# Decoder layer with a sparse memory attention: one more quarter of a step's weights computed on ScalarE

## What is computed

```python
def entmax15(x):
    x = (x - max(x)) / 2
    ...                                  # tau: the threshold for which the weights sum to 1
    return square(clip(x - tau, 0))
...
Q = layernorm(hidden) @ Wq.T
for _ in range(3):
    scores = einsum("bhsd,hnd->bhsn", xi, K) * beta
    w = entmax15(scores)
    xi = einsum("bhsn,hnd->bhsd", w, V)
out = xi @ Wo.T
x = layernorm(x + attn(x)); x = layernorm(x + xattn(x, ctx)); x = layernorm(x + ffn(x))
```

## Time and profile before

| | |
|---|---|
| median of 3 runs | 906.6 us (906.1 to 909.6) |
| profiled execution | 906.5 us, span 904.6 us |
| PE busy | 834.2 us, 92% of the span |
| DVE busy | 794.6 us, 88% |
| ACT busy | 705.6 us, 78% |
| POOL busy | 494.3 us, 55% |
| chain that ended last | PE 65%, DVE 18%, ACT 7%, POOL 5% |

### The profile page before, as it was taken

The page is one execution under the profiler, slowest core; times in us unless marked ns, Lnnn a source line. Parts: engine busy times, 40 slices in busy tenths (PEclk is TensorE's granted clock), DMA queues, the critical chain, the costliest instruction groups (busy, mean ns, idle before and its releaser), DMA issues.

```text
span 904.6 us, 17069 instructions
## 1 busy us (share of the span) xinstructions
PE 834.2 (92%) x4958; PEld 719.5 (80%) x4958; DVE 794.6 (88%) x2051; ACT 705.6 (78%) x1691; POOL 494.3 (55%) x2306
## 2 busy tenths in 40 slices
PE   6999996899999999999999999999999997999961
PEld 5877785688888888888888888888888886887850
DVE  3699999999999999999999999999998998978431
ACT  3588897998888989878989697989697789866320
POOL 4133536664564656666656566575645557654423
PEclk9999999999999999999999999999999998999995
DMA  8900020000000000000000001000000000000000
GB/s 280 204 1 1 16 91 11 9 2 2 1 1 1 1 1 13 1 3 1 1 1 1 12 2 30 7 1 1 2 1 19 1 1 7 7 1 7 7 1 27
DMA packets 24212, 17.55 MB, mean 19 GB/s; under 512 B 11761, under 2 KB 23537, under 8 KB 23857
## 3 DMA queue, kind: packets, MB, share of 16 engines
q1 hardware_dynamic: 23872, 16.13, 6.3%
q0 software_dynamic: 240, 0.27, 0.2%
HBM read 14.30 MB, written 2.10 MB: 18 GB/s over the span
## 4 chain that ended last, share of the span: by engine, by line
PE 65%; DVE 18%; ACT 7%; POOL 5%; issue 3%; DMA 1%; SPq 0%; POOLq 0%
PE banks L1227 24%; PE banks L1250 11%; DVE moments L793 7%; PE banks L1238 6%; PE banks L1278 6%; PE banks L1311 4%; PE banks L1101 4%; DVE top L773 4%; ACT work L704 3%; PE banks L1287 3%; DVE work L813 2%; PE banks L1303 2%; ACT work L695 1%; ACT work L716 1%; PE banks L1324 1%
## 5 line engine op out<-in xcount | busy, mean ns | idle before, releaser
L793 DVE BATCH_NORM_STATS2 moments<-work 128x6 f32<-128x512 f32 x576 | 373.7, 686 | 5.8 <-ACT work L704 2.9
L704 ACT ACTIVATE work<-work,neg_u 128x256 f32<-128x256 f32 x768 | 329.1, 519 | 47.5 <-DVE neg_u L805 25.6
L1227 PE MATMUL banks<-weights_s,work 128*128 128x256 f32 x1536 | 350.7, 381 | 6.1 <-ACT work L695 4.2
L1227 PEld LDWEIGHTS banks<-weights_s,work 128*128 128x128 f32 x1536 | 286.9, 191 | 46.2 <-issue 7.6
L695 ACT ACTIVATE work<-banks,neg_low 128x256 f32<-128x256 f32 x384 | 152.7, 494 | 10.2 <-DVE neg_low L784 10.0
L923 POOL TENSOR_TENSOR resid_sum<-moments 128x8 f32<-128x8 f32 x144 | 30.7, 214 | 226.6 <-DVE moments L793 225.4
L773 DVE MAX8 top<-banks 128x8 f32<-128x256 f32 x384 | 141.7, 415 | 8.2 <-PE banks L1227 7.4
L716 ACT ACTIVATE work<-banks 128x512 f32<-128x512 f32 x192 | 112.9, 611 | 24.4 <-PE banks L1238 23.9
L1238 PE MATMUL banks<-ident,work 128*128 128x128 f32 x768 | 107.9, 276 | 15.0 <-DVE work L813 7.5
L1250 PE MATMUL banks<-weights_s,work 128*128 128x256 f32 x512 | 115.0, 380 | 0.3 <-ACT work L716 0.3
L1238 PEld LDWEIGHTS banks<-ident,work 128*128 128x128 f32 x768 | 86.2, 141 | 31.9 <-DVE work L813 16.1
(11 more groups left out here) (155 smaller groups left out, 1154.2 us busy)
## 6 DMA issues: line engine op xcount, KB each, us to landing
work<-in_L_xattn_Wo_dram SPq DMA_DIRECT2D x2, 1024.0 KB, 11.0
out_dram<-work SPq DMA_DIRECT2D x16, 128.0 KB, 1.7
work<-in_L_xattn_w_kc_q_dram SPq DMA_DIRECT2D x2, 768.0 KB, 5.5
rows<-in_L_xattn_Wq_dram SPq DMA_DIRECT2D x1, 1536.0 KB, 13.8
rows<-in_x_dram SPq DMA_DIRECT2D x1, 1536.0 KB, 7.1
work<-in_L_attn_Wq_dram SPq DMA_DIRECT2D x1, 1024.0 KB, 10.3
work<-in_L_attn_Wo_dram SPq DMA_DIRECT2D x1, 1024.0 KB, 13.6
work<-in_ctx_dram SPq DMA_DIRECT2D x32, 32.0 KB, 2.2
```

What stands on the lines that cost most here:

```text
L704: ins = nc.scalar.activation(q_resid[:, j, h, :], q_resid0[:, j, h, :], ACT.Relu, bias=small["neg_u"][:, j, h:h + 1])
L793: ins = nc.vector.bn_stats(moments[:, j, 2 * q:2 * q + 2, :].rearrange("p h k -> p (h k)"), r.rearrange("p h n -> p n h"))
L1227: ins = nc.tensor.matmul(ps_scores[:, h, :], lhsT, w[:, h, t, :], start=(t == 0), stop=(t == CT - 1))
```

## The change

A constant `DVE_WEIGHTS = 2` takes the place of the fixed three. DVE computes the quarters 0 and 1 of the weights (heads 0 to 3), ACT the quarters 2 and 3 (heads 4 to 7), in one stage `last_weights` of four instructions with a signal after each quarter. PE waits for the third quarter on ACT's semaphore. The strings of all engines are replaced; that of DVE is 48 entries shorter (one for each of 16 tiles and 3 steps). Lines behind the new constant are three higher, and behind `last_weights` four.

```diff
+DVE_WEIGHTS = 2
...
-        dve += four("weights", s)[:3]
+        dve += four("weights", s)[:DVE_WEIGHTS]
...
-        "SP": "3015249876304ac2db157f6e89abdecf",
+        "SP": "023156741a92806c3bef45d78ac9bedf",
...
-            RESID_STEP = (EVALS - 1) * QUARTERS + 1
+            RESID_STEP = EVALS * QUARTERS - DVE_WEIGHTS
...
                         act.wait_ge(u_ready[j], eval_count(p, s, EVALS - 1))
-                        for h in (6, 7):
+                        for h in range(2 * DVE_WEIGHTS, HEADS):
                             ins = nc.scalar.activation(q_resid[:, j, h, :], q_resid0[:, j, h, :], ACT.Relu,
                                                        bias=small["neg_u"][:, j, h:h + 1])
-                        ins.then_inc(resid_ready[j], 1)
+                            if h % 2:
+                                ins.then_inc(resid_ready[j], 1)
...
-                        if q < 3:
-                            pe.wait_ge(weights_ready[j], p * (STEPS * 3) + (s * 3 + q + 1))
+                        if q < DVE_WEIGHTS:
+                            pe.wait_ge(weights_ready[j], p * (STEPS * DVE_WEIGHTS) + (s * DVE_WEIGHTS + q + 1))
                         else:
-                            pe.wait_ge(resid_ready[j], resid_count(p, s, EVALS, 1))
+                            pe.wait_ge(resid_ready[j], resid_count(p, s, EVALS, q - DVE_WEIGHTS + 1))
```

More of the change, by code:

```diff
@@ L177, in tile_turns @@
     return {
[L178 to L211, removed]
@@ new lines, in tile_turns @@
+        "ACT": "hhhhhhhh01h000000h02101h110h0h00hh2h2h1h11h100022h11011h02221h0h20h010121h0200120h2h11131h000211h021"
+               "21h333232h11h1303h33h1202h2023h33322h2h2100133331000042235000021233336020010373323211021132330300111"
+               "1220223111122203342444102304434142112442144330330204144555504343555005323422544455254453343431556266"
+               "6535661636801335515563646644456556567777461565777114467535166674754626669275547122445456766772575567"
+               "524a264424b77677643444667473474475355456367762776553535347375888748545588458866686843884999965647494"
+               "99987669c9988797878795665698896886777878885475887aaaa989867ada855a5a599e78899aa8aa97899967aa76a77999"
+               "898688596899bbbb8a88a9bbbbaaaa887bbb66b68689abaf8ba7ab8788999a9a8aa9a9996aac7c7cbbc9998bb797bcb7a7c9"
+               "cacbbbb9a8ac9c9aabbbb9ccaacba8bbaccddddc9c8aa8ad7d8cad8d8c8bccddddacc9bdac9caddaccccabbbbcc8eecee9db"
+               "bdb9ebae99e9e9bbbbdddedeaeebccadedbdbedebdbddcdcccda9ddeffffadadbffffaaafddffdfedfbcbeffccacefefebcb"
+               "ccfffcfbebebebecfffcfecceeedddcdeffeeffdedddbefcdfecdfceddeecdceeceeccdceeeeffedffdefeefddffceffdddd"
+               "ffffeeeffffeedfeeeefffffefffff",
@@ new lines, in tile_turns @@
+        "POOL": "hh0000101100112221120200010212101133303322211323hhhh200000202333003311113231212201124244442420140333"
+                "5355553444553243636604065656564145757713757665616176722444466044577744555727535327475588861666883456"
+                "96499889966997273778884787486a5aa885aa79997aa93958998885bbb878bb66aabab88aa9949a9a69698c77cc99bbbcc5"
+                "bbaaabaccb9ada7dd88addccacdd7cc6cc8babbeb8ee99bbeebdbdede9dd7ddbaf9ffaffcfcfccaacecedebbffccfeedd8df"
+                "eefdbdcffdbdeee9eccdeeeefcfffddaffecffdbedefeeffgcfefdf",
```

28 lines of the change are left out of this document (23 added, 5 removed).

## The result

| | before | changed |
|---|---|---|
| median, 4 runs each | 907.25 us (906.13 to 909.62) | 916.3 us (915.46 to 917.18) |
| ratio | | 1.0096 (95%: 1.0072 to 1.0120) |
| profiled execution, span | 906.5, 904.6 us | 915.5, 913.7 us |
| granted clock, whole span | 0.981 | 0.976 |

The account below looks back on a forecast made before the run. PE was taken as nearly full, held up in the middle mostly by DVE's long queue. The terms -3.4 + 2.5 - 0.6 - 2.7 - 1.4 = -5.6 took the profiled 906.5 us to 901 us, range 890 to 915.

Parts of the forecast that it names:

- ACT in the middle: From 200 to 700 us ACT's load rises from 86.2% to 91.8%, adding 2.5 us of PE waits.
- Moved entries: Rewritten lists of PE, ACT, POOL and SP, mostly moved by one to five entries, costed at nothing.
- the idle time moves by over 5 us at a place where weights play no part: Sign that the forecast is wrong and the rewritten lists, not the moved quarter, made the difference.
- The third quarter: PE's waits before third quarters (heads 4 and 5) in the middle go: -3.4 us, bounds 0 and -11.5.
- the five places: Five PE waits before a third quarter, from 277.48 to 657.19 us, 3.4 us together.
- the -0.6: The rest of PE's waits for DVE in the middle, 2.6 us, shrinks with DVE's load by 0.6 us.
- The start: From 50 to 200 us half of DVE's relief of 5.4 us reaches PE: -2.7 us.
- late: From 700 to 850 us a fifth of 7.5 us of POOL waits and lost clock is gained: -1.4 us.
- rival C: DVE's relief reaches further, idle share at start and late falls to the middle's: 886 us, chance 0.05.
- The durations: Expected profile: L817 x192 about 60 us, L714 x192 about 87; DVE about 765 us busy, ACT 749.
- B: Longer ACT blocks become PE's wait: 913 us, chance 0.24; sign: PE waits for ACT of over 10 us.
- A: Nothing to be felt, ACT's cost meets the third quarter's saving: 905 us, 902 to 911, chance 0.29.

Follow-up runs that it names:

- e1: The new split of two quarters on DVE and two on ACT, with the lists of the kernel before; 919.33 us, 1.0131.
- e8: The kernel before with DVE's third quarter left out, ACT's load and the lists unchanged; 903.75 us, 0.9969.
- e7: The kernel before with two unused relu added behind ACT's quarter in each of the 48 blocks; 919.35 us, 1.0162.
- e12: The kernel before with one unused relu added behind ACT's quarter in each block; 910.49 us, 1.0038.
- e13: The kernel before with ACT's fourth quarter left out, all lists unchanged; 908.31 us, 1.0017.
- e14: The changed kernel with the third quarter left out on ACT, so new lists with two quarters on DVE and one on ACT; 915.81 us, 1.0103.
- e2: The old split of three quarters on DVE and one on ACT, with the changed kernel's lists; 926.0 us, 1.0202.
- e9: The kernel before with five third quarters that PE waited for moved right behind their second on DVE; 906.73 us, 0.9997.
- e10: The kernel before with the third quarter of five steps that PE waited for computed on ACT instead of DVE; 907.45 us, 1.0004.
- e3: The changed kernel with tile 11's softmax sums and tile 12's second quarter moved earlier in DVE's list; 917.35 us, 1.0115.
- e6: The changed kernel with ACT's block of four split in two entries, the first square between them; 933.51 us, 1.0317.
- e11: The kernel before with two unused relu per step added behind ACT's fourth square instead of in the block; 920.48 us, 1.0146.

## Why the prediction was wrong

The time of 916.3 us lies outside the range of 890 to 915. Step by step:

- **"ACT in the middle", +2.5.** This is the term that failed first. Without the moved entries, the prediction's terms are worked out on the order of before, and their sum is -5.6; e1 is that kernel and took 12.1 us more than before (919.33 against 907.26). The gains were put at 8.1 us and came to 2.9 (e8). The load on ACT was put at 2.5 in the middle and at nothing elsewhere. It cost 12.7 us by the medians, 14.7 by the ratio (e7). In the middle alone, from PE's 1010th matmul to its 3952nd, e7's profiled execution took 509.9 us against 501.4, so the term of 2.5 measured 8.5; 3.8 us of waiting for the square that PE needs became 12.1 from 50 to 850 us. The value came from a line through two engines' busy shares and waits, which treats 91.8% as the cause of a wait. It isn't one: half the load cost a quarter (e12), 36 us less gave nothing (e13), and on the new lists the same load cost nothing that shows (e14). The line's two waits were also read low, from the two largest lines of each engine; over all lines of 200 to 700 us they are 4.1 us for ACT and 7.0 for DVE, which would have given +1.7, further off still.
- **"Moved entries. ... I cost them at nothing."** This step failed as well. At equal load the rewritten lists cost 12 us with 2 and 1 quarters (e14 against e8) and 18.7 with 3 and 1 (e2), and gave back 3 with the changed kernel's own 2 and 2 (e1 against the changed kernel). The step looked only at POOL and at transfers, and took "by one to five entries" for small. The rewrite did away with the price of ACT's load and put one of its own in its place, so the changed kernel is slow for another reason than e1. The prediction named a sign for this, "the idle time moves by over 5 us at a place where weights play no part". It came near: the waits outside the turn of the weights rose by 4.6 us, 4.1 of them for L772.
- **The third quarter, -3.4.** The wait was read rightly and it went, but the value is wrong. In the changed kernel ACT has all four relu of tile 10 done 19 us before PE gets there, and PE waits 0.34 us, for a square; no wait for the weights of a third quarter is left:

```profile
494.65 1.73 ACT L714 ACTIVATE work<-work,neg_u 128x256 f32<-128x256 f32 x4
...
515.83 1.11 PE L1242 MATMUL banks<-ident,work 128*128 128x128 f32 x8 [0.34 <-ACT work L720]
```

  At the five places together PE still waits 1.8 us ahead of the third quarter in the changed kernel, for the square or the copy that frees the bank, and 0.6 ahead of tile 6's second. Moved alone the five quarters give 0 (e9, e10); with the relief of DVE all 48 give 2.9 (e8), of which the middle shows 3.0 between the same two matmuls (498.4 us), where this term and the -0.6 had 4.0. The text had it as a bound, "0 (the next wait takes its place)", and that end was the true one for the places alone.
- **The start, -2.7, and late, -1.4.** Both wrong. In e8 PE's 1010th matmul starts at 201.0 us, against 200.3: the relief gives nothing in the start. From its 3952nd to its 4801st the relief gives 0.6 us (146.5 against 147.1). In the changed kernel the idle time from 50 to 200 us rose from 14.2 to 15.4, and late the clock fell to 0.95. The largest wait in each was known not to be for weights; that argument, put under rival C, spoke for setting these terms to nothing.
- **The durations.** L817 took 60.3 us for 60 forecast. L714 took 82.0 for 87: 0.427 us each in blocks of four, where the pairs had 0.455. DVE came to 773.0 us for 765 and ACT to 741.4 for 749: both moved by less than their groups (21.6 and 35.8 us against 29.7 and 38.4). None of this bears on the result.
- **The rivals.** B gave 913 us and the right sign, with a chance of 0.24. Its mechanism and its price (14.6 us, less the gains) are what the old lists show (e1, e7), but it isn't what holds the changed kernel, so that 913 is near 916.3 is luck. Its sign, waits for ACT of over 10 us, is met (6.7 + 3.6 + 1.3 = 11.6), but the kernel before had 9.2 of the same kinds and e14, with ACT's load gone, keeps the two larger lines at 9.2. It was no test. A and C are ruled out.
- **The skill.** The Trainium skill, ScalarE: Activation LUTs, section Rules for kernel authors, says of a relu "Use VectorE, not ScalarE", and the change goes against it. The trace agrees on the ranking of the durations, 0.427 against 0.314 us (82.0 and 60.3 us by 192), and the estimate of 0.40 us was near. The result has the rule's sign. With the old lists the added relu on ScalarE did cost 1.6% (e7); with the lists of the change they cost nothing that shows (e14), and that kernel is slow for another reason.

What stays open: which engine's list carries the 12 us of e14 against e8. Exchanging the list of one engine alone wasn't tried. PE's waits give a hint: ahead of a second quarter it waits 4.5 us for DVE's weight in e14, 0.2 in the kernel before. Nor is it shown that no good order exists for the new split; e1, the changed kernel and e3 to e6 are six orders, all slower than before, by 1.0 to 3.2%. In the old order the relief of DVE gives 0.3% (e8); by that estimate a third quarter on POOL, which wasn't tried either, would give no more there. No version here that computes all the weights beats the kernel before.

## What to carry to other kernels

Where each engine works through a fixed list, an engine's busy share doesn't say what its next microsecond costs: ACT was 78% busy, and 34.5 us more cost 13 to 15 us, half of that about 3, and 36 us less gave nothing. Price a move of work by running the two halves apart, the relief with the work left out and the load with a dummy added, before the order is rewritten; here these two runs show a gain of 0.3% and a cost of 1.6% on the old order. And when the change also rewrites the order, cross orders and loads in a table. The two need not add, and a table with one corner missing can name a cause that the other corner takes back: e14 alone says the order costs 1.3%, e1 that at the change's own load it costs nothing.

## What the runs showed of the hardware that was not expected

- A stall can be paid twice. The changed kernel's PE stands still 4.6 us longer and is busy 4.5 us longer for the same 4958 matmuls, while the granted clock is below 1.00 in 50 of the 100 us around its large waits (before in 20). Many short waits did not do this: e7's PE stands still 9.9 us longer (80.3 against 70.4), 8.3 of them in waits of at most 1.7 us for the square, and is busy only 2.0 us longer, with the clock of the span at 0.980 (before 0.981). In e11 PE is busy 841.9 us, 7.7 more than before, though no wait stands out; its clock of 0.977 accounts for about half of that, and the rest is not explained.
- One instruction more costs its engine less than its own time. A DVE weight of 128x256 has a mean of 362 ns in its row and 0.3125 us as its share of the group, since neighbours overlap, but 96 fewer took only 0.21 to 0.23 us each off DVE's busy time (e8: 20.5 us, the change: 21.6). This last figure is rough: with the same DVE instructions as before, e7 has DVE busy 4.2 us longer. An ACT one has 511 ns and 0.455, or 0.427 in blocks of four, and 96 more or fewer moved ACT by 0.36 to 0.38 each (e7: 34.5, the change: 35.8, e13: 36.4).
